# A graph-attention and mixture-of-experts layer: the first layer norm applied after the projection instead of before it

## The reference

```python
def _layernorm(x): m, v = mean(x), var(x); return (x - m) / sqrt(v + 1e-5)

# attention, per batch
Wh = einsum('bni,oi->bno', h, W)
si, sj = Wh @ a1, Wh @ a2
e = leaky_relu(si[:, :, None] + sj[:, None, :], 0.2)
attention = softmax(where(adj > 0, e, -9e15), axis=-1)
gnn = elu(einsum('bij,bjo->bio', attention, Wh))
# the layer
x = x + gnn(_layernorm(x), adj, W, a)
x = x + ffn(_layernorm(x), ...)   # router per batch, two of eight experts, gelu, layer norm at the end
```

## Time and profile before

| what | value |
|---|---|
| median of 3 runs | 370.45 us |
| lowest, highest run | 368.57, 370.85 us |
| profiled execution, first to last instruction | 368.4 us |
| PE busy | 279.6 us, 76% |
| DVE busy | 295.9 us, 80% |
| POOL busy | 258.3 us, 70% |
| ACT busy | 213.0 us, 58% |
| mean granted TensorE clock | 0.893 of full speed |

### The profile page before, as it was taken

One profiled execution on the slowest core, in us unless ns is written; L12 is line 12 of the kernel. 1 busy time (PEld: TensorE's weight loads), 2 busy tenths in 40 slices (PEclk: granted clock), 3 DMA queues, 4 the chain that ended last, 5 costly groups with the idle time before them and its releaser, 6 DMA issues. The chain is left out here.

```text
span 368.4 us, 7612 instructions
## 1 busy us (share of the span) xinstructions
PE 279.6 (76%) x1800; PEld 241.0 (65%) x1800; DVE 295.9 (80%) x806; ACT 213.0 (58%) x443; POOL 258.3 (70%) x457
## 2 busy tenths in 40 slices
PE   7598868487678769768677841499999998878970
PEld 3387757477567658657666741258999987867860
DVE  3988999967978978979779741556879999999995
ACT  3658958575785695688488831454655433544220
POOL 4848998988888988998899775214775654456431
PEclk9879978898898898899699985588999999999995
DMA  7634314134124314403300101223443233322111
GB/s 255 254 141 146 117 55 172 43 132 171 63 108 171 99 72 171 141 29 144 144 28 0 60 18 42 79 64 85 134 144 98 90 110 100 127 85 89 53 60 57
DMA packets 23479, 38.23 MB, mean 104 GB/s; under 512 B 2576, under 2 KB 15264, under 8 KB 21408
## 3 DMA queue, kind: packets, MB, share of 16 engines
q1 hardware_dynamic: 21152, 33.78, 26.5%
q10 hardware_dynamic: 2304, 4.20, 3.0%
HBM read 29.57 MB, written 4.19 MB: 92 GB/s over the span
## 5 line engine op out<-in xcount | busy, mean ns | idle before, releaser
L992 PE MATMUL banks<-whx,prob_t 128*128 128x129 f32 x512 | 71.6, 297 | 0.3 <-ACT prob_t L826 0.2
L992 PEld LDWEIGHTS banks<-whx,prob_t 128*128 128x128 f32 x512 | 68.7, 214 | 0.9 <-ACT prob_t L826 0.9
L826 ACT ACTIVATE prob_t<-banks 128x512 f32<-128x512 f32 x64 | 36.0, 591 | 39.5 <-PE banks L979 39.5
L537 DVE SCALAR_TENSOR_TENSOR logit<-masked_dst,shift_pos,leaky 128x512 f32<-128x512 f32 x64 | 47.1, 785 | 1.0 <-ACT leaky L799 0.5
L407 POOL TENSOR_SCALAR x2s<-x1s,nm,rstd 128x128 f32<-128x128 f32 x64 | 43.6, 692 | 3.5 <-POOL rstd L369 3.5
L369 POOL TENSOR_TENSOR rstd<-sums,minus_half 128x4 f32<-128x4 f32 x32 | 44.2, 1381 | 2.5
L799 ACT ACTIVATE leaky<-masked_dst,shift_neg 128x512 f32<-128x512 f32 x64 | 42.5, 717 | 4.8 <-DVE shift_neg L526 4.8
L979 PE MATMUL banks<-ident,logit 128*128 128x128 f32 x256 | 43.1, 308 | 2.4 <-DVE logit L537 1.7
L970 PE MATMUL banks<-ident,x2s 128*128 128x128 f32 x64 | 12.9, 337 | 39.6 <-POOL x2s L407 39.6
L504 DVE CUSTOM_DVE_ANT_0 masked_dst<-mask,banks 128x512 f32<-128x512 bf16 x64 | 40.0, 681 | 0.4 <-issue 0.4
L427 POOL TENSOR_TENSOR x2t_lo<-x2t_all,x2t_hi 128x512 fp32r<-128x512 f32 x16 | 24.0, 1498 | 20.4 <-ACT x2t_hi L884 20.4
(11 more groups left out here) (129 smaller groups left out, 657.3 us busy)
## 6 DMA issues: line engine op xcount, KB each, us to landing
adj_sb<-in_adj_dram SPq DMA_DIRECT2D x16, 1024.0 KB, 4.9
x_all<-in_x_dram SPq DMA_DIRECT2D x16, 256.0 KB, 4.9
x_all<-x2s SPq DMA_DIRECT2D x16, 256.0 KB, 2.3
w1s<-in_L_ffn_W_dram SPq DMA_DIRECT2D x32, 128.0 KB, 2.1
w2r<-in_L_ffn_W_dram SPq DMA_DIRECT2D x32, 128.0 KB, 2.1
out_dram<-prob_t ACTq DMA_DIRECT2D x16, 256.0 KB, 2.1
gnn_w_sb<-in_L_gnn_W_dram SPq DMA_DIRECT2D x1, 64.0 KB, 2.5
beta_less_one<-in_L_ffn_beta_dram SPq DMA_DIRECT2D x1, 64.0 KB, 7.2
```

The lines of the kernel that those rows point to most:

```text
L537: nc.vector.scalar_tensor_tensor(out=logit[:, t, :], in0=masked_dst[:, t, :], scalar=shift_pos[:, t:t + 1], in1=leaky[:, t, :], op0=ALU.ad ...
L826: nc.scalar.activation(prob_t[:, t, :], lt_ps[t % 2], ACT.Exp).then_inc(s_prob, 1)
L992: last = nc.tensor.matmul(av_ps[:, t, 0:D + 1], prob_t[:, t, c * P:(c + 1) * P], whx[par][:, c, 1:WHX], start=(c == 0), stop=(c == T - 1))
```

## The change

The norm is no longer applied to x ahead of the projection. DVE computes the centred weights once (`gnn_w_centred`, three operations). PE transposes raw x, which SP loads a second time into `x_rows` for this. The projection yields both scores and the rows in one product of 130 columns. ACT copies the result out of PSUM in four pieces and multiplies each row by its factor `rstd1`. The second score is column 0 of those rows, and a new PE function `spread_dst` spreads it over the partitions, between the last logit transposes and `attend` 1. POOL's first norm loses three of its ten operations and moves from n+3 to n+2. ACT loses the four `xn` operations. All else on DVE stays.

```diff
+                if in_range(half, n + 3) and not (isinstance(half, int) and 2 * half + n + 3 < 2):
+                    load_rows(half, n + 3)
...
+            def load_rows(half, n):
+                b, h, par = batch_at(half, n)
+                if not isinstance(half, int) or b >= 2:
+                    sp.wait_ge(s_xt_ps, b - 1)
+                    waits_met(sp)
+                sp.dma_start(x_rows[par][:], x_dram[b]).then_inc(s_xr[par], 16)
...
-            load_x(0, 0)
+            load_rows(0, 0)
...
+            load_x(0, 0)
+            load_rows(0, 1)
+            load_adj(0, 0)
             load_x(0, 1)
-            load_adj(0, 0)
...
-                nc.gpsimd.tensor_tensor(mr1[:], sums1[:, 0, :], rstd1[par][:], ALU.mult).then_inc(s_pch1, 1)
-                pool.wait_ge(s_pch1, base + 9)
-                waits_met(pool)
-                nc.gpsimd.tensor_scalar(nb1[par][:], mr1[:], -0.5, 0.0, ALU.mult, ALU.add).then_inc(s_rstd1, 2)
...
-                if in_range(half, n + 3):
-                    norm1_scalars(half, n + 3)
+                if in_range(half, n + 2):
+                    norm1_scalars(half, n + 2)
...
+            nc.vector.bn_stats(w_stats[:], gnn_w_sb[:]).then_inc(s_centre, 1)
+            dve.wait_ge(s_centre, 1)
+            nc.vector.bn_aggr(w_mean[:], w_stats[:]).then_inc(s_centre, 1)
+            dve.wait_ge(s_centre, 2)
+            nc.vector.tensor_scalar(gnn_w_centred[:], gnn_w_sb[:], w_mean[:, 0:1], None, ALU.subtract).then_inc(s_centre, 1)
...
-            def norm1(half, n):
-                b, h, par = batch_at(half, n)
-                act.wait_ge(s_rstd1, 2 * b + 2)
-                if not isinstance(half, int) or b >= 1:
-                    act.wait_ge(s_xt_ps, b)
-                for t in range(T):
-                    nc.scalar.activation(xn[:, t, :], x_all[:, b, t * D:(t + 1) * D], ACT.Identity,
-                                         bias=nb1[par][:, t:t + 1], scale=rstd1[par][:, t:t + 1]).then_inc(s_xn, 1)
...
-                nc.scalar.copy(whx[par][:, :, 0:D + 1], wh_ps[:, :, 0:D + 1]).then_inc(s_wh, 1)
+                act.wait_ge(s_pch1, 7 * b + 7)
+                waits_met(act)
+                for t in range(T):
+                    nc.scalar.activation(whx[par][:, t, 0:D + 2], wh_ps[:, t, 0:D + 2], ACT.Copy,
+                                         scale=rstd1[par][:, t:t + 1]).then_inc(s_wh, 1)
...
-                for t in range(T):
-                    pe.wait_ge(s_xn, T * b + t + 1)
-                    last = nc.tensor.transpose(tr_ps[:, t * P:(t + 1) * P], xn[:, t, :], ident[:])
+                pe.wait_ge(s_xr[par], 16 * h + 16)
+                for t in range(T):
+                    last = nc.tensor.transpose(tr_ps[:, t * P:(t + 1) * P], x_rows[par][:, t, :], ident[:])
...
-                nc.tensor.matmul(dst_ps, dst_weights[:], xnt[:], start=True, stop=True).then_inc(s_dst, 1)
...
+            def spread_dst(half, n):
+
+                b, h, par = batch_at(half, n)
+                pe.wait_ge(s_wh, T * b + T)
+                if not isinstance(half, int) or b >= 1:
+                    pe.wait_ge(s_md, T * b)
+                for t in range(T):
+                    last = nc.tensor.matmul(dst_ps[:, t * P:(t + 1) * P], whx[par][:, t, 0:1].to_broadcast([P, P]),
+                                            ident[:], start=True, stop=True)
+                last.then_inc(s_dst, 1)
...
                     for t in range(T):
                         if t + 2 < T:
                             transpose_logits(half, n, t + 2)
+                        if t == 1 and in_range(half, n + 1):
+                            spread_dst(half, n + 1)
                         attend(half, n, t)
```

More of the change, by code:

```diff
@@ L76, in gat_moe_kernel @@
         whx = [sb(f"whx{i}", [P, T, WHX]) for i in range(2)]
+        x_rows = [sb(f"x_rows{i}", [P, T, D]) for i in range(2)]
         masked_dst = sb("masked_dst", [P, T, N])
@@ L90, in gat_moe_kernel @@
         rstd1 = [sb(f"rstd1_{i}", [P, T]) for i in range(2)]
-        mr1 = sb("mr1", [P, T])
-        nb1 = [sb(f"nb1_{i}", [P, T]) for i in range(2)]
         bn2 = [sb(f"bn2_{i}", [P, T, 6]) for i in range(2)]
@@ L138, in early @@
                 return attention.enter_context(nc.sbuf_tensor(name, shape, F32))
-            xn = early("xn", [P, T, D])
+            early("spare_rows", [P, T, D])
             h_att = early("h_att", [P, T, D])
@@ L351, in moments @@
             def moments(bn, sums, rstd, chain, base, scaled_mean=None):
-                nc.gpsimd.tensor_tensor(sums[:, 0, :], bn[:, :, 1], bn[:, :, 4], ALU.add).then_inc(chain, 1)
+                if scaled_mean is not None:
+                    nc.gpsimd.tensor_tensor(sums[:, 0, :], bn[:, :, 1], bn[:, :, 4], ALU.add).then_inc(chain, 1)
                 nc.gpsimd.tensor_tensor(sums[:, 1, :], bn[:, :, 1], bn[:, :, 4], ALU.subtract).then_inc(chain, 1)
                 nc.gpsimd.tensor_tensor(sums[:, 2, :], bn[:, :, 2], bn[:, :, 5], ALU.add).then_inc(chain, 1)
-                pool.wait_ge(chain, base + 2)
+                first = 3 if scaled_mean is not None else 2
+                pool.wait_ge(chain, base + first - 1)
                 nc.gpsimd.tensor_tensor(sums[:, 3, :], sums[:, 1, :], sums[:, 1, :], ALU.mult).then_inc(chain, 1)
-                pool.wait_ge(chain, base + 4)
+                pool.wait_ge(chain, base + first + 1)
                 waits_met(pool)
@@ L365, in moments @@
                     nc.gpsimd.tensor_scalar(scaled_mean, sums[:, 0, :], -0.5, 0.0, ALU.mult, ALU.add).then_inc(chain, 1)
-                pool.wait_ge(chain, base + 6)
+                pool.wait_ge(chain, base + first + 3)
                 nc.gpsimd.tensor_tensor(sums[:, 1, :], sums[:, 2, :], sums[:, 3, :], ALU.add).then_inc(chain, 1)
-                pool.wait_ge(chain, base + (8 if scaled_mean is not None else 7))
+                pool.wait_ge(chain, base + (8 if scaled_mean is not None else 6))
                 nc.gpsimd.tensor_tensor(rstd, sums[:, 1, :], minus_half[:], ALU.pow).then_inc(chain, 1)
@@ L510, in row_bound @@
                 dve.wait_ge(s_md, T * b + T)
-                nc.vector.tensor_tensor(z_max[:], whx[par][:, :, 0], dst_max[:], ALU.add).then_inc(s_dch, 1)
+                nc.vector.tensor_tensor(z_max[:], whx[par][:, :, 1], dst_max[:], ALU.add).then_inc(s_dch, 1)
             def row_maximum(half, n):
@@ L583, in step @@
                 if in_range(half, n):
-                    dve.wait_ge(s_wh, batch_at(half, n)[0] + 1)
+                    dve.wait_ge(s_wh, T * batch_at(half, n)[0] + T)
                 if in_range(half, n + 1):
@@ L849, in step @@
                     copy_wh(half, n + 1)
-                if in_range(half, n + 2):
-                    norm1(half, n + 2)
                 if in_range(half, n):
```

56 lines of the change are left out of this document (27 added, 29 removed).

## The result

The changed kernel takes 390.38 us (median of 4 runs, 389.31 to 391.74), beside 370.65 us for the kernel before in the same comparison: a ratio of 1.0515, 95% interval 1.0458 to 1.0572. The prediction was 369.0 us with a range of 359 to 382. It was wrong, by 21 us, and on the wrong side. Where some runs of one kernel lie over 1.5% above its fastest, as in experiments 3, 5 and 10, the shorter ones are the ones to compare with.

What follows compares the result with a forecast made beforehand. POOL was taken to bound the kernel before. Fourteen steps of 12.7 us, less the last three's savings, give 173.2 us after a first `inv_sum` at 32.4: 1.5 us saved, 369.0 us, range 359 to 382.

Steps and rivals of the forecast that it cites:

- A step of 12.6 us: POOL's attention step: own work falls to 8.6 us, plus 4.0 us lost to DVE; bounds 10.6 and 14.7.
- the third rival: POOL stays the bound as `x2s` falls under DVE's logits: 13.2 us a step, 376 us; chance 0.13.
- The copies and the spread: ACT's four scaled copies out of PSUM take 1.13 us, PE's four float32 spread products 1.05 us.
- M = I + 6.0: DVE's `masked_max` starts (M) 6.0 us after `inv_sum` starts (I), behind the spread that ends at I + 5.6.
- 0.7 us for clock and hops: Added to each 12.0 us step for PE's low clock after its pause and the ACT-PE-DVE hop; ends 0 and 1.6.
- DVE's wait for the spread: Before `masked_max`, 0.2 to 1 us each step; more than 1 us would show the forecast wrong.
- 6.0 + 2.73 + 3.27: DVE's step: `inv_sum` to `masked_max`, on to `z_max`, on to the next `inv_sum`; 12.0 us.
- The sum of the steps: Fourteen steps between `inv_sum` rows: 14 x 12.7 us, less 3 x 0.87 and 2.0 for the last three: 173.2 us.
- The start: Extra loads delay the first `z_max` to 16.6 us, the second to 28.9, the first `inv_sum` to 32.4 instead of 28.05.
- The end: Everything behind the last but one `inv_sum` (last attention, `norm2`, router, experts) was called untouched.
- Moving the first norm from n+3 to n+2 costs nothing: In POOL's queue: free, because `copy_wh` needs the norm's factor one step later than POOL makes it.
- The low clock: Rival: PE's low clock falls on the new path each step, adding 1.6 us: 13.6 us a step, 382 us; chance 0.20.

Runs made afterwards that it cites:

- experiment 3: Changed kernel with two idle PE products of 512 columns ahead of each projection, in PE's long pause: 384.64 us, ratio 1.0368 to the kernel before.
- experiment 5: Changed kernel with POOL's `x1b_all` written in four operations of 128 columns instead of one of 512: 387.43 us, ratio 1.0341 to the kernel before.
- experiment 10: experiment 6 with `x1b_all` moved behind the first norm on POOL: 365.13 us, ratio 0.9861 to the kernel before.
- experiment 2: Changed kernel with ACT copying `whx` ahead of the first two probability tiles and PE spreading right behind the second logit transposes: 367.14 us, ratio 0.988.
- experiment 1: Changed kernel with POOL's `x1b_all` moved behind the first norm: 379.6 us, ratio 1.0223 to the kernel before.
- experiment 7: Kernel before the change, with only `x1b_all` moved behind the first norm on POOL: 369.61 us, ratio 0.994.
- experiment 6: experiment 2 without the two idle products of the second `warm_up`: 366.36 us, ratio 0.9857 to the kernel before.
- experiment 8: experiment 6 with `x1b_all` in four pieces of 128 columns: 374.65 us, ratio 1.0076 to the kernel before.

## Why the prediction was wrong

**POOL: right.** A step of 12.6 us was forecast. POOL is not the bound in the changed kernel; in experiment 2, where it is, eleven full steps average 12.45 us and those in the middle of the run take 12.5 to 12.9. The three small operations have gone, and `x2s`, which the third rival put wholly under the logits, does fall there in experiment 2 (4.33 us). The step is 12.45 us all the same; where the loss is made up was not looked into.

**The copies and the spread: right in size.** 1.13 us was forecast for the copies and 1.14 measured, 1.05 and 1.06 for the spread.

**The step "M = I + 6.0": nearly right.** M is I + 6.47 in the step shown and I + 6.72 on average, the 6.7 that it makes with the 0.7 us for clock and hops. But DVE's wait for the spread, 0.2 to 1 us by the forecast, is 1.6 us on average, over the 1 us that the prediction named as a sign of being wrong: DVE is there sooner than I thought, and the spread is not. What was wrong is what I made of it: I called the price 0.2 us at the full clock, compared with a forecast of POOL, and never asked how much lies between this place of the spread and an earlier one. Experiments 1 and 2 give it, in spans: 376.6 against 364.9, some 12 us, in the start, each step and the end.

**The step "6.0 + 2.73 + 3.27": the failed term.** `z_max` to `inv_sum` was taken as 3.27 us, from a step of the kernel before. It is 4.65 us in the step shown and 4.49 on average, because `x1b_all` meets one of the four small operations. POOL has become faster and DVE later, and that moved the end of the second norm from the mask and the `masked_max` to the bound and the shifts. The working treated the losses between the two engines as POOL's alone, 4.0 us, "because DVE's mask, logits and residuals stay", and looked for meetings with long DVE operations only. A short one in the way of a long POOL instruction loses most in proportion: 1.3 us for 0.16. Experiment 1 shows it, and experiment 7 shows that it comes with the change. With `x1b_all` out of the way the term is 3.45 us and a full step 12.90, near the forecast of 12.7. This term is worth about 11 of the 21 us; the rest lies in the start and the end and in the last three steps, below.

The rule that was weighed in the prediction points at it. The Trainium skill, page "SBUF — State Buffer", section "Who interferes with whom", excludes a GpSimd instruction that reads SBUF and a DVE instruction with two SBUF inputs from each other for the whole instruction. All four small operations have two SBUF inputs, while `masked_max` takes one of its two from PSUM. The runs agree on both: 1.31 us beside `x1b_all` for `shift_neg`, 0.69 us beside it for `masked_dst` in experiment 2. I used the rule for POOL's side of the sum and not for DVE's.

**The sum of the steps.** Full steps average 13.87 us against 12.7 (eleven of them, +12.9 us), and the last three take 38.2 us against 33.5 (+4.7): 17.6 of the 23.0 us by which the span missed its 366.9. The 4.6 us taken off the last three steps for their missing `stats1` and mask were too much in every version: in experiment 2 those steps take 36.1 us, only 1.3 less than three full ones.

**The start: the path right, the load misread.** 32.4 was forecast for the first `inv_sum`, 33.88 came. From the first `z_max` to the second it takes 12.19 us (12.3 was forecast) and from there 3.53 us to `inv_sum` (3.5); the excess is all in the first `z_max`, at 18.16 us instead of 16.6. The load behaved otherwise than I worked out. I had the load of batch 2 later by 1.9 us in front of the first mask. The diff puts the load of batch 1 behind `adj`, so its statistics, which began at 5.48 us before, wait for it until 9.63 (10.80 in experiment 6), and the first mask stands behind them, at 10.42 (11.59) instead of 9.00. In the changed kernel PE is later still: its first transposes stand behind the second `warm_up`, which takes 3.74 us in this trace. With the same products at 1.96 us, in experiment 5, the first `z_max` comes at 16.16 and the first `inv_sum` at 31.90, a little ahead of the forecast. "Hide under the first loads", I said of the three operations on the weights; they made PE pause for 0.39 us ahead of its first transpose. That the pause made the idle products long is not shown, and the 1.96 us behind such pauses in experiments 3 and 5 speak against it.

**The end: wrong.** "Untouched" was wrong by 2.75 us. The last step has no mask to hide behind, so the late shifts reach ACT's `leaky`, the logits start late, and the last attention runs alone. Its last rows in the changed kernel:

```profile
223.40 1.31 DVE L540 SCALAR_TENSOR_TENSOR shift_neg<-whx,row_max 128x4 f32<-128x4 f32 x1
224.63 0.17 DVE L562 RECIPROCAL inv_sum<-banks 128x4 f32<-128x4 f32 x1
224.75 2.56 ACT L805 ACTIVATE leaky<-masked_dst,shift_neg 128x512 f32<-128x512 f32 x4 [4.54 <-DVE shift_neg L540]
...
235.58 0.18 DVE L562 RECIPROCAL inv_sum<-banks 128x4 f32<-128x4 f32 x1 [4.83 <-PE banks L1004]
```

With the early spread that stretch is 7.94 us (8.20 before), and with `x1b_all` moved but the spread late it is 9.90. The remaining 1.2 us behind the last `inv_sum` were not looked into.

**"Moving the first norm from n+3 to n+2 costs nothing": right in the changed kernel, wrong as a statement.** It is free while DVE is late. In experiment 2 DVE waits 12.2 us at the place that the move made tighter.

**The rivals.** The low clock gave the right side of the result by the wrong cause: its 1.6 us a step were not needed, and in experiment 3 the steps with a stretched small operation are no shorter at the higher clock.

## What to carry to other kernels

When a change makes one engine faster, write down which of its long instructions will then run beside which instructions of its neighbour, the shortest ones too, and price both sides; a stretched short instruction hides in busy time and in no list of waits, so compare the mean duration of equal groups in the two traces. When a value that one engine waits for is now made by a longer chain, its place in every queue of that chain is part of the change: here the same arithmetic took 390 us with the spread behind the last logit transposes and 367 us with it, and the copy that it needs, in front of them. And test such a change in both places before judging it, since the gain of one part can show only once the other part is right.

## What the runs showed of the hardware

- A DVE instruction on 4 columns, 0.16 us by itself, takes 1.11 to 1.31 us when it begins within 0.17 us of a POOL `tensor_tensor` of 512 columns, 1.26 us, and 0.79 us when it begins 0.49 us behind it; each time it ends with it. In the step shown `shift_neg` began 0.03 us ahead of `x1b_all` and was held all the same; POOL's `x2s` was still running then, until 112.92 us, so the row doesn't say that the one to begin first lost.
- Four POOL instructions of 128 columns in place of one of 512 took 1.69 us instead of 1.26 beside the small operations, and over a run 38.3 us instead of 20.2 (experiment 5) and 30.7 instead of 21.6 (experiment 8). Cutting a POOL instruction up did not free DVE: in the step shown two small operations take 0.40 and 0.49 us, and the mask 2.35 instead of 1.99.
- PE's two idle products of 512 columns (four instructions) took 3.74 us behind a pause of 0.39 us in the changed kernel, 1.96 us behind pauses of 0.33 and 0.97 us in experiments 3 and 5, and 1.88 us without a pause before. The granted clock is 1.00 in all four stretches, so neither the pause nor that clock shows the cause, which stays open.
- The granted clock of a step goes to 0.50 after the pause of 4.0 us ahead of the projection (8 products, 2.07 us), and the projection, the first logit transposes and a part of what follows run at that level. Experiment 3 lifts the clock of 100 to 212 us from 0.86 to 0.91, and an estimate of 3.4 of its 11.7 us is what it leaves for that.
